# One recurrence stage on one core: a bias sum that carries its own step size, and a new order of the products on TensorE

## The reference, cut to what matters

```python
def step(carry, inp):
    W1c, b1c = carry
    xq, xk, xv, et = inp
    Z1 = xk @ W1c + b1c
    grad = _ln_l2_bwd(Z1, xv - xk, g, bb)
    Attn1 = jnp.tril(xq @ xk.swapaxes(-1, -2))
    b1_bar = b1c - jnp.tril(et) @ grad
    Z1_bar = xq @ W1c - et * Attn1 @ grad + b1_bar
    last_eta = et[..., -1, :, None]
    W1n = W1c - (last_eta * xk).swapaxes(-1, -2) @ grad
    b1n = b1c - (last_eta * grad).sum(-2, keepdims=True)
    return ((W1n, b1n), xq + _ln(Z1_bar, g, bb, EPS_IN))
...
return _ln(out, post_w, post_b, EPS_IN) @ o_w.T
```

## Time and profile before

| | us |
|---|---|
| median of 3 runs | 6555.11 (6519.12 to 6576.57) |
| the profiled execution | 6570.32, its span 6568.5 |
| TensorE busy | 5831.2 (89% of the span) |
| VectorE busy | 4090.7 (62%) |
| ScalarE busy | 2173.4 (33%) |
| GpSimd busy | 2140.4 (33%) |

### The profile page before, as it was taken

The page is one execution under the profiler, slowest core; times in us unless marked ns, Lnnn a source line. Parts: engine busy times, 40 slices in busy tenths (PEclk is TensorE's granted clock), DMA queues, the critical chain, the costliest instruction groups (busy, mean ns, idle before and its releaser), DMA issues. The chain is left out here.

```text
span 6568.5 us, 136994 instructions
## 1 busy us (share of the span) xinstructions
PE 5831.2 (89%) x39482; PEld 4065.8 (62%) x39482; DVE 4090.7 (62%) x14673; ACT 2173.4 (33%) x6003; POOL 2140.4 (33%) x3398
## 2 busy tenths in 40 slices
PE   1799999999598898999988988998789999599999
PEld 0344444444377777777777777777666666367777
DVE  5566666665467666766777677667656666544444
ACT  0111111111244444444444444444333333233433
POOL 0244444444233333333333333333211222122222
PEclk9899999999588888888888889888899999799999
DMA  6233333333334343433444344334332221112221
GB/s 234 83 114 128 128 120 123 126 122 119 117 102 108 105 107 105 109 104 106 107 109 107 106 107 115 104 101 111 85 119 83 83 83 65 64 71 89 92 94 66
DMA packets 823380, 692.97 MB, mean 105 GB/s; under 512 B 357400, under 2 KB 758176, under 8 KB 811840
## 3 DMA queue, kind: packets, MB, share of 16 engines
q1 hardware_dynamic: 732480, 542.55, 27.7%
q10 hardware_dynamic: 90240, 142.75, 5.8%
HBM read 402.97 MB, written 282.20 MB: 104 GB/s over the span
## 5 line engine op out<-in xcount | busy, mean ns | idle before, releaser
L1390 PE MATMUL proj_ps<-proj_w_sb,proj_h 128*128 128x512 f32 x3072 | 1345.5, 596 | 0.0
L1390 PEld LDWEIGHTS proj_ps<-proj_w_sb,proj_h 128*128 128x128 f32 x3072 | 577.2, 190 | 743.4 <-issue 716.6
L2170 PE MATMUL scan_ps_y<-scan_o_t,proj_wo_sb 128*128 128x128 f32 x4096 | 666.6, 313 | 1.5 <-DVE scan_y L1963 0.9
L1312 DVE SCALAR_TENSOR_TENSOR proj_lin<-proj_ps,proj_rstd,proj_wbias_sb 128x512 f32<-128x512 f32 x384 | 284.4, 747 | 536.1 <-PE proj_ps L1390 535.1
L2170 PEld LDWEIGHTS scan_ps_y<-scan_o_t,proj_wo_sb 128*128 128x128 f32 x4096 | 565.3, 214 | 64.4 <-issue 23.0
L1736 POOL TENSOR_TENSOR scan_stored<-scan_core,scan_rate 128x128 f32<-128x128 f32 x512 | 332.7, 650 | 665.0 <-DVE scan_core L1947 665.0
L1785 ACT ACTIVATE scan_square<-scan_ps_z 128x64 f32<-128x64 f32 x1024 | 219.8, 220 | 946.6 <-PE scan_ps_z L2090 946.6
L1926 DVE TENSOR_TENSOR scan_zg<-scan_ps_z,scan_gain 128x128 f32<-128x128 f32 x512 | 146.0, 285 | 582.5 <-ACT scan_square L1785 578.7
L1729 POOL TENSOR_TENSOR scan_rate<-scan_rstd,scan_record 128x2 f32<-128x2 f32 x512 | 100.8, 197 | 1147.3 <-DVE scan_rstd L1929 1147.2
L2102 PE MATMUL scan_ps_w<-scan_step,scan_record 64*128 64x128 f32 x4088 | 438.4, 343 | 4.3 <-DVE scan_step L1952 4.3
L2161 PE MATMUL scan_ps_out<-scan_q_t,scan_k_t 64*128 64x128 f32 x2048 | 201.6, 350 | 209.1 <-DVE scan_zn L2016 209.1
(11 more groups left out here) (288 smaller groups left out, 12256.4 us busy)
## 6 DMA issues: line engine op xcount, KB each, us to landing
scan_record<-records SPq DMA_DIRECT2D x1032, 98.0 KB
records<-proj_rec ACTq DMA_DIRECT2D x128, 784.0 KB, 3.6
scan_k_in<-records SPq DMA_DIRECT2D x266, 128.0 KB, 2.8
spectra<-fourier_spec SPq DMA_DIRECT2D x16, 2112.0 KB, 6.4
fourier_spec<-spectra SPq DMA_DIRECT2D x16, 2112.0 KB, 8.1
stats_x<-x SPq DMA_DIRECT2D x16, 2048.0 KB, 8.2
proj_h<-x SPq DMA_DIRECT2D x32, 1024.0 KB, 7.4
queries<-proj_q ACTq DMA_DIRECT2D x128, 256.0 KB, 3.7
```

Of the source, the lines that this page charges most:

```text
L1312: v.scalar_tensor_tensor(lin[q][:, n], ps[q][n][:], rstd[k][:, j:j + 1], T.wbias[:, n], ALU.mult, ALU.add).then_inc(lin_sb.sem, 1)
L1390: last = pe.matmul(ps[j % 2][n][:], h[k][:, ct, j * P:(j + 1) * P], T.w[:, n, ct], start=ct == 0, stop=ct == CT - 1)
L2170: done = pe.matmul(ps_y[:, n], T.wo[:, ct, n * P:(n + 1) * P], o_t[:, ct], start=ct == 0, stop=ct == CT - 1)
```

## The change

Three things are changed, all in `scan_and_read`.

First, the bias. `b_sum` now starts from the bias itself (`first` x `b0`, put there once at the start) and adds `b_step` = `core` x step size of the last token. So `project_k` no longer needs the `b0` product, and `heads` is a plain 0/1 matrix. The one remaining bias product is issued as four products of 32 columns instead of one of 128. GpSimd has one operation more per chunk and group (`b_step`), ahead of `stored`. In the read-out, `ones` is plain and the product uses 64 rows of `b_sb` instead of 17.

Second, ScalarE's `squares` copies `ps_out` to `zo` in two halves and squares `zo`; VectorE makes `zn` from `zo` in one operation; `tile_weights` waits for `zo` instead of `zn`.

Third, TensorE's order within a pair.

```diff
@@ gpsimd: gradients
-                v.tensor_tensor(rate_pair[g][:], rate[g][:].unsqueeze(2).broadcast_to([P, PB, 2]),
-                                pair_last[:].unsqueeze(1).broadcast_to([P, PB, 2]), ALU.mult).then_inc(rate_sb[g].sem, 1)
+                v.tensor_tensor(rate_last[g][:], rate[g][:].unsqueeze(2).broadcast_to([P, PB, 3]),
+                                pair_last[:].unsqueeze(1).broadcast_to([P, PB, 3]), ALU.mult).then_inc(rate_sb[g].sem, 1)
...
+                v.tensor_tensor(b_step[g][:], core[g][:], rate_last[g][:, :, 2:3].broadcast_to([P, PB, HD]),
+                                ALU.mult).then_inc(b_step_sb[g].sem, 1)
...
+                v.tensor_tensor(b_sum[g][(c + 1) % RING][:], b_step[g][:], b_sum[g][c % RING][:], ALU.add
+                                ).then_inc(b_sum_sb[g].sem, 1)
...
                 v.tensor_tensor(stored[g][c % 2][:], core[g][:], rate[g][:].unsqueeze(2).broadcast_to([P, PB, HD]),
                                 ALU.mult).then_inc(stored_sb[g].sem, 1)
...
-                v.tensor_tensor(b_sum[g][(c + 1) % RING][:], stored[g][c % 2][:], b_sum[g][c % RING][:], ALU.add
-                                ).then_inc(b_sum_sb[g].sem, 1)
@@ scalar: squares
-                act.wait_ge(hsq_sb.sem, hsq_sb.at(t, 0))
+                act.wait_ge(zn_sb.sem, zn_sb.at(t, 0))
                 for n in range(2):
                     act.wait_ge(out_ps.sem, out_ps.at(t, n + 1))
-                    a.activation(zsq[:].rearrange("p (a n) e -> p a n e", n=2)[:, :, n], ps_out[n][:, :, 0:HD], ACT.Square
-                                 ).then_inc(zsq_sb.sem, 1)
+                    a.copy(zo[:].rearrange("p (a n) e -> p a n e", n=2)[:, :, n], ps_out[n][:, :, 0:HD]).then_inc(zo_sb.sem, 1)
+                act.wait_ge(hsq_sb.sem, hsq_sb.at(t, 0))
+                act.wait_ge(zo_sb.sem, zo_sb.at(t, 2))
+                a.activation(zsq[:], zo[:], ACT.Square).then_inc(zsq_sb.sem, 1)
@@ vector: head_norms
-                for n in range(2):
-                    done = v.tensor_tensor(zn[:].rearrange("p (a n) e -> p a n e", n=2)[:, :, n], ps_out[n][:, :, 0:HD],
-                                           hrstd[:].rearrange("p (a n) -> p a n", n=2)[:, :, n:n + 1].broadcast_to([P, HP, HD]), ALU.mult)
-                done.then_inc(zn_sb.sem, 1)
+                v.tensor_tensor(zn[:], zo[:], hrstd[:].unsqueeze(2).broadcast_to([P, NH, HD]), ALU.mult).then_inc(zn_sb.sem, 1)
@@ tensor: project_k, tile_weights
-                pe.matmul(ps_z[g][:, 0:F], ind[:], b0[:].rearrange("p b e -> p (b e)"), start=True, stop=False, skip_group_check=True)
                 pe.wait_ge(b_sum_sb[g].sem, b_sum_sb[g].at(s, 0))
-                pe.matmul(ps_z[g][:, 0:F], heads[:], b_sum[g][at.c % RING][:].rearrange("p b e -> p (b e)"), start=False, stop=False,
-                          skip_group_check=True)
+                for a in range(HP):
+                    pe.matmul(ps_z[g][32 * a:32 * a + 32, 0:F], heads[:, 32 * a:32 * a + 32],
+                              b_sum[g][at.c % RING][:].rearrange("p b e -> p (b e)"), start=True, stop=False, skip_group_check=True)
...
-                pe.wait_ge(zn_sb.sem, zn_sb.at(t, 0))
+                pe.wait_ge(zo_sb.sem, zo_sb.at(t, 0))
@@ tensor: body
+                update_last = scan and not (isinstance(at.s, int) and at.s == 0)
+
                 if scan:
                     project_k(0, at)
                 if at.odd:
+                    if kq:
+                        tile_query_turn(kq, proj)
                     if proj:
                         tile_project(proj, 1)
-                elif out:
-                    tile_bias_and_state(out)
-                if scan and not (isinstance(at.s, int) and at.s == 0):
-                    update(1, before)
-                if at.odd:
-                    if proj:
                         tile_project(proj, 2)
                 else:
                     if proj:
                         tile_outputs_turn(proj)
                     if out:
-                        tile_weighted(out)
+                        tile_bias_and_state(out)
+                if update_last:
+                    update(1, before)
                 if scan:
                     project_k(1, at)
                 if at.odd:
                     if kq:
                         tile_weights(kq)
+                    if proj:
+                        tile_project(proj, 3)
                     if scan:
-                        if kq:
-                            pe.wait_ge(q_t_sb.sem, q_t_sb.at(kq[0], 1))
                         turn_keys(at.v * 8 + at.slot + B)
-                elif proj:
-                    tile_project(proj, 0)
+                else:
+                    if out:
+                        tile_weighted(out)
+                    if proj:
+                        tile_project(proj, 0)
                 if scan:
                     update(0, at)
-                if at.odd:
-                    if proj:
-                        tile_project(proj, 3)
-                elif kq:
-                    tile_query_turn(kq, proj)
```

More of the change, by code:

```diff
@@ L1452, in scan_and_read @@
         rate = each("rate", [P, PB])
-        rate_pair = each("rate_pair", [P, PB, 2])
+        rate_last = each("rate_last", [P, PB, 3])
+        b_step = each("b_step", [P, PB, HD])
         square = sb("square", [P, GR, PB, HD])
@@ L1551, in scan_and_read @@
         out_ps = one("out_ps", 2)
-        zsq_sb = one("zsq_sb", 2)
+        zo_sb = one("zo_sb", 2)
+        zsq_sb = one("zsq_sb")
         hsq_sb = one("hsq_sb")
@@ L1570, in scan_and_read @@
         block = ctx.enter_context(nc.Block())
-        loads = 18
+        loads = 13
         class Place:
@@ L1608, in _ @@
         def _(sp):
-            for dst, src in ((gain8, d["gain_rows"]), (heads, d["heads"]), (ind, d["ind"]), (ends, d["ends"]), (w0_in, d["w0"]),
+            for dst, src in ((gain8, d["gain_rows"]), (heads, d["heads"]), (first, d["first"]), (w0_in, d["w0"]),
                              (b0_in, d["b0"]), (pair_in, d["pairs"]), (masks_in, d["masks"]), (read_eps, d["eps"])):
@@ L1914, in _ @@
             steps.then(dve, v.memset(ones[:], 1.0))
-            steps.then(dve, v.tensor_scalar(ones[:], ones[:], weight[:], None, ALU.mult))
             dve.sem_inc(init, 1)
+            dve.wait_ge(first_ps, 1)
+            for g in range(GR):
+                for b in range(PB):
+                    steps.then(dve, v.tensor_copy(b_sum[g][0][:, b], ps_z[0][:, 0:HD]))
+            dve.sem_inc(first_sb, 1)
             def gradients(at, g):
@@ L2065, in _ @@
             made.then_inc(start_ps, 1)
+            pe.matmul(ps_z[0][:, 0:HD], first[:], b0[:], start=True, stop=True).then_inc(first_ps, 1)
+            pe.wait_ge(first_sb, 1)
             def turn_keys(count):
@@ L2459, in shape_constants @@
         "heads": heads.T @ heads,
-        "ind": heads,
-        "ends": np.stack([np.arange(P) % 64 == 0, np.arange(P) % 64 != 0], 1),
+        "first": heads * np.tile(np.repeat(np.eye(CS)[0], 2), NH // 2),
         "tok_inv": np.tile(1.0 / np.arange(1, CS + 1, dtype=np.float32), NH),
```

53 lines of the change are left out of this document (23 added, 30 removed).

## The result

The changed kernel takes 6790.18 us (median of 4 runs, 6784.46 to 6800.17), the kernel before 6565.84 (4 runs): ratio 1.0356, 95% interval 1.030 to 1.0412. It is slower, as forecast, by 224 us where 363 were forecast. The profiled execution took 6800.17 us with a span of 6798.0, 229.5 more than before.

What follows compares the result with a forecast made beforehand. TensorE's list, its work, waits and clock, was taken to bound the stage. Products -1.85, waits +1.7 and clock +3.1 gave +2.95 us in each of 123 pairs, +363 us on 6570, so 6930 us, range 6700 to 7200.

Steps and rivals of the forecast that it cites:

- The wait for `zn`: Ahead of line 2161: TensorE's wait of 1.67 us a pair goes, since `tile_weights` now needs only `zo`.
- Transposes ahead: After each even chunk's first Z1, TensorE stands 1.7 us until ScalarE has made `on` for the transposes.
- The keys' copy: Behind `turn_keys`, TensorE waits 1.25 us once a pair for ScalarE's copy of the state, queued after `keys_out`.
- Nothing between update and Z1: At the three other places, TensorE waits 0.35 us each for the state's copy, 1.05 us a pair.
- The wait ahead of line 2082: Wait of 0.25 us a pair ahead of line 2082 goes, because a longer wait stands ahead of it.
- The waits together: TensorE's waits in a pair become 4.0 us in place of 2.3, +1.7 us.
- The bias products: In Z1, four 32-column products take 0.37 us in place of 0.83, saving 1.85 us a pair; sign: under 0.4 us.
- The clock: Falls in every pair through the even chunk, costing 5.8 us in place of 2.5; +3.1 taken; sign: stage below 0.75.
- The sum: Whole kernel: -1.85 + 1.7 + 3.1 = +2.95 us in each of 123 pairs, +363 us, about 6930 us.
- The clock does no worse than now: Rival for the stage: falls move but their price stays 2.5 us a pair; 6550 us, chance 0.15.
- The clock stays at 2.4 GHz: Rival for the stage: pauses of 1.7 us don't lower the clock; pair 20.25 us, 6245 us, chance 0.14.
- No overlap: Rival for Z1's bias products: column products don't overlap, +2.9 us a pair, about 7290 us, chance 0.07.

Runs made afterwards that it cites:

- fill_both: Changed kernel plus useless TensorE products, six ahead of the wait for `on`, four ahead of the even chunk's first bias products; 6269 us, ratio 0.9561.
- fill_elsewhere: Changed kernel plus ten useless products in the odd chunk ahead of group 1's Z1, where TensorE is dense; 7081 us, ratio 1.082.
- turn_back: Changed kernel with the transposes of `on` put back behind group 1's update; 6437 us, ratio 0.9809 to the kernel before.
- old_order: Changed kernel with TensorE's order put back as in the kernel before, bias and `zo` edits kept; 6496 us, ratio 0.9926.
- cover: turn_back with projection part 3 again between the odd chunk's update and the next Z1; 6281 us, ratio 0.9607 to the kernel before.
- fill_on_only: Changed kernel plus six useless products ahead of the wait for `on` alone; 6309 us, ratio 0.962 to the kernel before.

## Why the prediction was right, point by point

- **What bounds.** TensorE's list with its clock, in both kernels of the comparison: fill_both and fill_elsewhere change nothing but that list and move the time by -521 and +291 us.
- **The wait for `zn`.** Gone, as said.
- **Transposes ahead.** Said 1.7 us in each of 123 pairs; measured 1.76 in the pair shown and 1.8 in 120. turn_back shows that it is the costliest single move.
- **The keys' copy.** Said 1.25; measured 1.27 at 2.4 GHz.
- **Nothing between update and Z1.** Said 0.35 at three places; measured 0.33, and all but hidden where the clock is low (0.1 us ahead of line 2092 at 3216.28). The copies of the state came to 188.3 + 23.6 us, 1.7 a pair in place of 2.3.
- **The wait ahead of line 2082.** Said to go. It didn't: it stands ahead of line 2086 with 42.7 us, 0.3 a pair. This step of the prediction was wrong, and small.
- **The waits together.** Said 4.0 us in place of 2.3, less 0.4 for the shrinking that I had put under the clock. Measured as TensorE's idle time in the stage, 493 against 286 us, they are 3.85 a pair in place of 2.24, +1.6.
- **The bias products.** Said 0.37 in place of 0.83. Where the state was there already, four column products take less, 3111.53 - 3111.31 = 0.22 us in the timeline of old_order:

```profile
3111.31 0.43 PE L2086 MATMUL scan_ps_z<-scan_b_sum,scan_heads 128*32 128x128 f32 x8 [3.99 <-issue]
3111.53 0.43 PE L2092 MATMUL scan_ps_z<-scan_state_snap,scan_k_t 128*32 128x64 f32 x16
```

  In the changed kernel Z1 mostly waits for the copy, and the block then takes its own 0.43 us ahead of the wait, a little over the 0.4 that I had named as a sign: 0.40 us saved in a Z1, 1.6 in a pair, for the 1.85 of the sum.
- **What was not in the sum.** Sorting products of one shape together saves time at an unchanged clock. Two projection parts in a row take 3226.81 - 3224.93 = 1.88 us, not 2 x 1.09; the transposes ahead of them 0.50, not 0.59; part 3 ahead of `turn_keys` about 0.99; `turn_keys` 0.53. About 0.55 us a pair. Lines 2119 and 2123 of fill_both, the products of 2114 and 2118, take 3012.15 - 3011.61 = 0.54 us and 0.84, where they took 0.63 and 0.95: another 0.2.
- **The clock.** Said to fall in every pair; there are 123 falls in the 128 pairs. Said to cost 5.6 us in place of 2.5. With products of 18.1 - 1.6 - 0.55 - 0.2 = 15.75 us and waits of 3.85, the pair of 24.6 us leaves 5.0 for the clock: +2.5 against the +3.1 said. This is what is left over and not a measurement of its own.
- **The sum.** -2.35 + 1.6 + 2.5 = +1.75 us, and 24.6 - 22.8 = 1.8 is what it has to make, since the clock's term is the rest. The forecast of +2.95 was too high by 0.5 in the products, by 0.1 in the waits and by 0.6 in the clock. The mechanism and the sign were right; the size was over by six tenths. The sign that I had named for the clock, below 0.75 in the stage, came narrowly, at 0.73.
- **The rivals.** "The clock does no worse than now" would have given 6550; the clock did worse, 0.73 against 0.84. "The clock stays at 2.4 GHz" would have given 6245; held there by fill_both the kernel takes 6269. The number was good, its condition wasn't met. The Trainium skill ("TensorE: Matmul & The Clock Gate", section "Why this matters for your kernels") warns only of pauses longer than these, so by it they should be harmless; fill_both and fill_elsewhere together show that here they are not, and the measurement decides. "No overlap" is refuted by 0.22 us for four products.

## What to carry to other kernels

When TensorE's list is the bound, price each move by what stands behind the wait it opens, not by the wait alone: here 1.8 us of standing ahead of a run of narrow products cost more in clock than in waiting (turn_back, 217 us against 116). Keep two waits apart (turn_back against cover), and leave a piece of independent work between a product and the use of a copy of its result; cover, with the two other edits kept, came to 3.9% under the kernel before by two such moves. Waits that can't be removed may be cheaper ahead of dense, whole-array work, behind which the clock came back; no run tests this by itself. Filling a stand with useless products is a quick way to measure what the clock costs, but put there and only there: elsewhere, or where the stand isn't there in every pair, the same products are pure loss.

## What I had not expected of the hardware

- Adding ten products of 128x128 by 128 columns to a pair made it 4.2 us shorter, 24.6 to 20.4 (fill_both).
- A stand of 1.3 us alone lowered the clock in none of 107 cases (fill_on_only), and one of 0.5 to 0.75 us alone in none of 21 (cover), but the two together, with 0.4 us of products between, in 52 of 73 (turn_back). In the changed kernel's pair shown it then stayed at 0.50 through 11.5 us with TensorE busy for 11.41 of them.
- Products of one shape in a longer run are cheaper: eight products of 128x128 by 128 columns in a row take 1.88 us, the same eight in two separate groups 2.18.
